# Mixing by pairs of output channels, and every transpose copied out of PSUM by ScalarE, in the first pass of a spectral convolution kernel

## Chip, cores and metric

One core of a Trainium2 chip. The metric is the time of one execution on the device in microseconds; the median of several executions is compared.

## The reference, cut to what matters

The input x is 16 images of 64 channels of 256 x 256, float32. Two layers follow each other, each a residual. Only the first layer matters here:

```
v    = groupnorm(x)                       # 32 groups of 2 channels
f    = rfft2(v)[..., :32, :17]            # only 32 x 17 modes are used
core = einsum('bhixy,hioxy->bhoxy', f, w) # 4 heads, 16 -> 16 channels per mode, complex
x    = x + irfft2(core padded with zeros) + bias
```

The second layer (a hyperbolic batch norm over channels) is computed in two further passes over x, which the change does not touch.

## The kernel before, in words

The kernel makes three passes over x. The first (`stage_a`) reads each image once, takes the 32 x 17 modes of every channel by matrix products, mixes them by the weights, and keeps the sums that the norms need. The second and third (`stage_b`, `stage_c`) read x again. Each pass is a block of its own: the next one starts when the engines have finished the one before.

**Tiles and slots.** An image is Q = 8 tiles of 8 channels (2 from each head), 2 MB each, loaded by SyncE (SP) into four buffers `xt`. For tile q of image b TensorE (PE) works in *slots*. Slot (b, q) is: the row transform of tile q (`row_dft`, L249, two halves i = 0, 1 of 8 matmul records each, into `p_rows[i]`); the transposes of tile q-1 (`transposes`, L262, two halves into `p_tr[i]`); and the column transform of tile q-2 (`col_dft`, L274, into `p_cols`). Slot (b, 2) has two more steps: the first sums of image b-1 (L284, L285) before its column transform, and the second sums of image b-2 (L292, L293) after it.

**ScalarE (ACT)** takes each tile in the order of its program: squares of heads 0 and 1 (L330), copy of `p_rows[0]` (L337), squares of head 2, copy of `p_tr[1]` of the tile before (L345), squares of head 3, copy of `p_rows[1]`. After tile 7 `keep` copies the sums of squares (L362). All engines execute their own program in order.

**VectorE (DVE)** runs, in `entry(b)`, for each q: copy of `p_tr[0]` of a later tile (`copy_tr`, L385), copy of `p_cols` of tile q of image b (L391), and the mixing of *image b-1* for two output channels (`mix`): two products of 128 x 1088 (L397) and two sums over 32 (L402). After q = 7 come `finish(b-1)` (L410 to L416: energies, which release the second sums on PE), `copy_tr(b+1, 1)`, `first_norm(b)` (waits for the first sums), `second_norm(b-1)` (waits for the second sums), and `start(b)` (L467 to L476: the normalised modes `xh` of image b), at whose end `mean_sum(b-1)` (L445 to L448) waits for two powers that GpSimd (POOL, L533, L534) computes from `second_norm`'s result.

**Who waits for whom.** `transposes(b, q)` half i waits until the copy of the tile before out of `p_tr[i]` is done (`tr_sb[i]`) and for `rows_sb`; `row_dft` half i waits for the copy of that half of the tile before; `col_dft` waits for both copies of its tile, and for the copy of `p_cols` two tiles back. `store_modes` stands in SP's queue between the loads of tiles 3 and 4 and waits for `finish`. The last image's mixing (8 times `mix`, `finish`, `second_norm`, `mean_sum`) runs on DVE alone when all else in the pass is done.

Of the kernel before, what the change touches and what calls it, by code (L numbers as in the profile page):

```python
# [20 lines left out]
ALU = mybir.AluOpType  # L21
ACT = mybir.ActivationFunctionType
AX_X = mybir.AxisListType.X
# [4 lines left out]
HEADS, CI = 4, 16  # L28
KX, KY = 32, 17
M2 = 2 * KY  # L30
# [64 lines left out]
def is_at(b, n):  # L95

    return isinstance(b, int) and b == n
# [47 lines left out]
def stage_a(nc, ctx, io, B):  # L145
# [3 lines left out]
    Q = C // 8  # L149
# [5 lines left out]
    tr_mm, tr_sb = sem("tr_mm"), [sem(f"tr_sb{i}") for i in range(2)]  # L155
    cols_mm, cols_sb = sem("cols_mm"), sem("cols_sb")
    sq_done, sq_kept = sem("sq_done"), sem("sq_kept")
    sums_mm, energy, stat_mm = sem("sums_mm"), sem("energy"), sem("stat_mm")
    y_ready, y_out, st_ready, st_out, chain = sem("y_ready"), sem("y_out"), sem("st_ready"), sem("st_out"), sem("chain")
# [4 lines left out]
    with ExitStack() as mem:  # L164
        sb = lambda n, s, d=FP32: mem.enter_context(nc.sbuf_tensor("a_" + n, s, d))
# [9 lines left out]
        wm = sb("wm", [128, CI, 2, CI * M2])  # L175
# [5 lines left out]
        xm = sb("xm", [128, CI, M2])  # L181
        xk = sb("xk", [128, CI, M2])
        xh = sb("xh", [128, KY, 2 * CI])
        prod = [sb(f"prod{k}", [128, 2, CI * M2]) for k in range(2)]
        y = sb("y", [128, CI, YS])
        yrot = sb("yrot", [128, CI, YS])
        t1, t2 = sb("t1", [128, CI, M2]), sb("t2", [128, CI, M2])
# [137 lines left out]
        @block.scalar  # L325
        def _(act):
            def squares(b, q, h):
                if not (is_at(b, 0) and q == 0 and h < 2):
                    act.wait_ge(sq_done, b * 32 + 4 * q + h - 1)
                nc.scalar.activation(junk[h % 2][:].rearrange("p (i w) -> p i w", i=2), xt[q % NX][:, h], ACT.Square,  # L330
                                     accum_out=sq[:, q, h:h + 1]).then_inc(sq_done, 1)

            def copy_rows(b, q, i):
                act.wait_ge(rows_mm, b * 16 + 2 * q + i + 1)
                if not (is_at(b, 0) and q < 2):
                    act.wait_ge(tr_mm, b * 16 + 2 * q + i - 3)
                nc.scalar.activation(rows[q % 2][i][:], p_rows[i][:], ACT.Copy).then_inc(rows_sb, 1)  # L337

            def copy_tr(b, q):
                if q < 0:  # L340
                    b, q = b - 1, q + Q
                act.wait_ge(tr_mm, b * 16 + 2 * q + 2)
                if not (is_at(b, 0) and q < 2):
                    act.wait_ge(cols_mm, b * 8 + q - 1)
                nc.scalar.activation(cols[q % 2][1][:], p_tr[1][:], ACT.Copy).then_inc(tr_sb[1], 1)  # L345

            def tile(b, q):
                act.wait_ge(x_in[q % NX], b * 64 + (q // NX) * 32 + 32)
                squares(b, q, 0)
                squares(b, q, 1)  # L350
                copy_rows(b, q, 0)
                squares(b, q, 2)
                if not (is_at(b, 0) and q == 0):
                    copy_tr(b, q - 1)
                squares(b, q, 3)
                copy_rows(b, q, 1)

            def keep(b):
                act.wait_ge(sq_done, b * 32 + 32)
                if not is_at(b, 0):  # L360
                    act.wait_ge(sums_mm, b)
                nc.scalar.activation(sqk[:], sq[:], ACT.Copy).then_inc(sq_kept, 1)  # L362
                act.wait_ge(sq_kept, b + 1)

            for q in range(Q):
                tile(0, q)
            keep(0)
            with act.Fori(1, B) as b:
                for q in range(Q):
                    tile(b, q)  # L370
                keep(b)
            copy_tr(B - 1, Q - 1)

        @block.vector
        def _(dve):
# [1 line left out]
            row = lambda k, n=16: sm[:, k, 0:n]  # L377
            pair = lambda a: a.rearrange("p (g i) -> p g i", i=2)
            V = nc.vector

            def copy_tr(b, q):
                dve.wait_ge(tr_mm, b * 16 + 2 * q + 1)
                if not (is_at(b, 0) and q < 2):
                    dve.wait_ge(cols_mm, b * 8 + q - 1)
                V.tensor_copy(cols[q % 2][0][:], p_tr[0][:]).then_inc(tr_sb[0], 1)  # L385

            def copy_cols(b, q):
                dve.wait_ge(cols_mm, b * 8 + q + 1)
# [4 lines left out]
            def mix(q, waited=None):  # L393


                for o in (2 * q, 2 * q + 1):
                    ch.inc(V.tensor_tensor(prod[o % 2][:], wm[:, o], xh[:].rearrange("p k n -> p (k n)").unsqueeze(1).to_broadcast((128, 2, CI * M2)), ALU.mult))  # L397
                ch.wait()
                for o in (2 * q, 2 * q + 1):
                    if waited is not None and o == 0:  # L400
                        dve.wait_ge(y_out, waited)
                    ch.inc(V.tensor_reduce(y[:, o, 0:M2].rearrange("p (a k) -> p a k", a=2), prod[o % 2][:].rearrange("p a (k n) -> p a k n", k=KY), AX_X, ALU.add))  # L402
                ch.wait()

            def finish(b):

                bc = lambda k: mode_w[:, k].unsqueeze(1).to_broadcast((128, CI, M2))
                if not is_at(b, 0):
                    dve.wait_ge(yrot_out, b * 16)
                V.tensor_scalar(yrot[:, :, 0:KY], y[:, :, KY:M2], misc[:, 5:6], None, ALU.mult).then_inc(y_ready, 1)  # L410
                V.tensor_scalar(yrot[:, :, KY:M2], y[:, :, 0:KY], misc[:, 6:7], None, ALU.mult).then_inc(y_ready, 1)
                ch.inc(V.tensor_tensor(t1[:], y[:, :, 0:M2], bc(0), ALU.mult))
                ch.step(V.tensor_tensor(t2[:], xk[:], bc(1), ALU.mult))
                ch.step(V.tensor_tensor(t1[:], t1[:], t2[:], ALU.add))
                ch.step(V.tensor_tensor(t1[:], t1[:], y[:, :, 0:M2], ALU.mult))
                V.tensor_reduce(row(8), t1[:], AX_X, ALU.add).then_inc(energy, 1)  # L416
# [25 lines left out]
            def mean_sum(b):  # L442
                dve.wait_ge(st_ready, b * 2 + 2)

                ch.step(V.scalar_tensor_tensor(out=row(17, 8), in0=row(13, 8), scalar=0.5, in1=pair(st[:, 0])[:, :, 0], op0=ALU.mult, op1=ALU.mult))  # L445
                a = pair(row(20))
                ch.inc(V.tensor_tensor(a[:, :, 0], a[:, :, 0], row(17, 8), ALU.add))
                ch.step(V.tensor_tensor(a[:, :, 1], a[:, :, 1], row(17, 8), ALU.subtract))  # L448
# [16 lines left out]
            def start(b):  # L465

                ch.inc(V.tensor_copy(row(2, 8), row(26, 8)))  # L467
                ch.inc(V.tensor_copy(row(3), row(27)))
                ch.step(V.tensor_copy(xk[:], xm[:]))
                dve.wait_ge(rstd1_ready, b + 1)  # L470
                ch.inc(V.tensor_tensor(xh[:].rearrange("p k (g j) -> p g j k", j=4), xk[:].rearrange("p i m -> p (i m)").rearrange("p (g j k) -> p g j k", j=4, k=KY),
                                       row(22, 8).unsqueeze(2).unsqueeze(3).to_broadcast((128, 8, 4, KY)), ALU.mult))
                ch.step(V.tensor_tensor(row(7, 8), row(4, 8), row(22, 8), ALU.mult))
                ch.step(V.tensor_scalar(row(7, 8), row(7, 8), misc[:, 4:5], None, ALU.mult))
                dcs = pair(xh[:, 0, 0::2])
                ch.step(V.tensor_tensor(dcs, dcs, row(7, 8).unsqueeze(2).to_broadcast((128, 8, 2)), ALU.add))  # L476
                if not is_at(b, 0):
                    mean_sum(b - 1)

            ch.inc(V.memset(row(20), 0.0))  # L480
            ch.inc(V.memset(y[:, :, M2:YS], 0.0))
            ch.inc(V.memset(yrot[:, :, M2:YS], 0.0))
            dve.wait_ge(const_in, 32 + 16 * 8)
            copy_tr(0, 0)
            for q in range(Q):
                copy_tr(*((0, q + 1) if q + 1 < Q else (1, 0)))
                copy_cols(0, q)
                if q == 5:
                    dve.wait_ge(w_in, 16)
                    neg = wm[:, :, 0].rearrange("p o (n r) -> p o n r", r=2)[:, :, :, 1]  # L490
                    ch.inc(V.tensor_scalar(neg, neg, -1.0, None, ALU.mult))
# [2 lines left out]

            def entry(b, last=False):
                for q in range(Q):
                    if q and not (last and q + 1 == Q):
                        copy_tr(*((b, q + 1) if q + 1 < Q else (b + 1, 0)))
                    copy_cols(b, q)
                    mix(q, None if is_at(b, 1) or q else (b - 1) * 16)  # L500
                finish(b - 1)
                if not last:
                    copy_tr(b + 1, 1)
                first_norm(b)
                second_norm(b - 1)
                start(b)

            copy_tr(1, 1)
            entry(1)
            with dve.Fori(2, B - 1) as b:  # L510
                ch.loop(b, 2, PER_A)
# [2 lines left out]
            entry(B - 1, last=True)  # L514
            for q in range(Q):
                mix(q, None if q else (B - 1) * 16)
            finish(B - 1)
            second_norm(B - 1)
            mean_sum(B - 1)
# [33 lines left out]
            pool.wait_ge(macc_out, 16)  # L553


PER_A = 63

TB = 4096
TC = 2048
# [823 lines left out]
```

## Time and profile before

| what | value |
|---|---|
| median of 3 runs | 3675.0 us (3665.37 to 3679.16) |
| profiled execution, its own time | 3669.49 us |
| its span (first to last instruction) | 3667.9 us |
| PE / DVE / ACT busy over the span | 2923.4 (80%) / 2747.2 (75%) / 2096.8 us (57%) |
| first pass ends, second begins | 1131.7 us |
| products of the mixing, L397 | 256 of 1283 ns |
| sums of the mixing, L402 | 256 of 1281 ns |

The span is 1.6 us shorter than the execution's own time. Busy shares are averages over three passes with different limits; only the first pass is touched. In the rows below the start of an instruction (or of a merged run of alike ones, "xN") comes first, then its length, both in microseconds; what stands in brackets is the idle time of the engine before it and what ended it. PE's L249, L262 and L274 are each one run per slot, so that a slot can be read off as the distance between two L249 rows.

### The profile page before, as it was taken

How to read it: one execution, taken by the hardware profiler on the slowest of the kernel's cores; microseconds unless marked ns; L12 is line 12 of the kernel's file. 1: busy time of each engine (PE TensorE's matmuls, PEld its weight loads, DVE VectorE, ACT ScalarE, POOL GpSimd, SP SyncE). 2: the span in 40 equal slices, each digit the busy share in tenths (PEclk: the TensorE clock that was granted, in tenths of full speed). 3: DMA queues.
4: the chain of work that ended last, by engine and by line, in shares of the span. 5: the costliest groups of instructions: out<-in, count | busy, mean ns of one | idle time of the engine just before them, and what ended most of it. 6: DMA issues, size and time to landing. Idle time of an engine off the chain costs nothing. (4 is left out here: it accounts for less than half of the span.)

```text
span 3667.9 us, 70122 instructions
## 1 busy us (share of the span) xinstructions
PE 2923.4 (80%) x26018; PEld 1461.4 (40%) x26018; DVE 2747.2 (75%) x2984; ACT 2096.8 (57%) x2866; POOL 1512.5 (41%) x862
## 2 busy tenths in 40 slices
PE   6998888989843766776775498898888899888887
PEld 3555555555521221222221344444444444444443
DVE  1888888888886546544564398888888888888888
ACT  5776676767720011101111388787777787777787
POOL 0101011010111111111111287787777777777778
PEclk9998888988866888887787699999999999999999
DMA  9877767777716989999996599999999999999998
GB/s 379 298 265 258 277 244 290 258 277 274 248 64 224 400 326 391 400 397 387 403 399 221 177 391 382 380 376 374 371 368 368 368 378 376 370 381 373 370 386 341
DMA packets 293210, 1211.32 MB, mean 330 GB/s; under 512 B 35266, under 2 KB 49799, under 8 KB 210695
## 3 DMA queue, kind: packets, MB, share of 16 engines
q1 hardware_dynamic: 263526, 1152.42, 82.5%
q0 software_dynamic: 14112, 43.37, 3.6%
q10 hardware_dynamic: 15360, 12.60, 1.2%
q8 instruction: 148, 2.42, 0.3%
q14 instruction: 64, 0.52, 0.0%
HBM read 883.89 MB, written 324.31 MB: 329 GB/s over the span
## 5 line engine op out<-in xcount | busy, mean ns | idle before, releaser
L1309 POOL TENSOR_TENSOR c_ot<-c_ot,c_pp 128x1024 f32<-128x1024 f32 x512 | 1213.6, 2372 | 411.2 <-DVE c_ot L1262 410.0
L1252 DVE SCALAR_TENSOR_TENSOR c_xt<-c_xt,keep_k,c_p_u 128x1024 f32<-128x1024 f32 x512 | 653.7, 1277 | 135.8 <-PE c_p_u L1132 109.5
L1262 DVE SCALAR_TENSOR_TENSOR c_ot<-c_p_f,keep_k,c_xt 128x1024 f32<-128x1024 f32 x512 | 657.3, 1284 | 108.3 <-DMA out<-c_ot 59.8
L1206 ACT ACTIVATE c_pp<-c_p_p,keep_cols 128x1024 f32<-128x1024 f32 x512 | 570.7, 1115 | 259.8 <-PE c_p_p L1144 258.7
L1132 PE MATMUL c_p_u<-c_mv,c_zc 64*128 64x256 f32 x4096 | 595.6, 410 | 78.9 <-DVE c_xt L1252 76.9
L1213 ACT ACTIVATE c_sq<-c_xt,keep_cols 128x1024 f32<-128x1024 f32 x512 | 583.1, 1139 | 63.9 <-DVE c_xt L1252 63.6
L330 ACT ACTIVATE a_junk<-a_xt 128x1024 bf16<-128x1024 f32 x512 | 537.1, 1053 | 29.1 <-DMA a_xt<-in_x 21.8
L249 PE MATMUL a_p_rows<-a_xt,a_dft_h 128*64 128x512 f32 x2048 | 516.3, 650 | 32.8 <-DMA a_bias_t<-in_bias 18.1
L1132 PEld LDWEIGHTS c_p_u<-c_mv,c_zc 64*128 64x128 f32 x4096 | 361.1, 190 | 362.7 <-issue 219.5
L528 POOL TENSOR_TENSOR a_sm<-a_sm 128x8 f32<-128x8 f32 x16 | 26.7, 1670 | 929.4 <-DVE a_sm L463 929.4
L1144 PE MATMUL c_p_f<-c_rt,keep_lw 64*128 64x512 bf16 x1024 | 315.3, 388 | 104.6 <-DVE c_ot L1262 95.8
L667 PE MATMUL b_p_al<-b_xt,b_awc 128*32 128x512 f32 x2048 | 290.0, 642 | 95.7 <-DMA b_xt<-in_x 95.7
L402 DVE TENSOR_REDUCE a_y<-a_prod 128x34 f32<-128x1088 f32 x256 | 317.5, 1281 | 5.7
L1144 PE MATMUL c_p_p<-c_rt,keep_lw 64*128 64x512 bf16 x1024 | 318.5, 392 | 0.0
L397 DVE TENSOR_TENSOR a_prod<-a_wm,a_xh 128x1088 f32<-128x1088 f32 x256 | 317.9, 1283 | 0.3
L1155 PE MATMUL c_p_t<-c_sq,c_hw 128*32 128x512 f32 x2048 | 289.3, 638 | 1.3 <-ACT c_sq L1213 1.3
L828 DVE TENSOR_TENSOR b_prod<-b_spt,b_arow 64x2176 f32<-64x2176 f32 x16 | 38.7, 2418 | 330.1 <-DMA b_spt<-spec 330.0
L725 ACT ACTIVATE b_dn<-b_dn,b_minus 128x512 f32<-128x512 f32 x16 | 11.6, 722 | 478.3 <-DVE b_dn L853 478.3
L667 PE MATMUL b_p_ls<-b_xt,b_awc 128*32 128x512 f32 x2048 | 279.5, 621 | 0.0
L1118 PEld LDWEIGHTS c_p_z<-c_idft,c_ys 128*37 128x37 f32 x7936 | 232.2, 114 | 106.0 <-issue 106.0
L1118 PE MATMUL c_p_z<-c_idft,c_ys 128*37 128x64 f32 x7936 | 271.2, 221 | 0.0
L274 PE MATMUL a_p_cols<-a_dft_w,a_cols 128*128 128x34 f32 x2048 | 264.4, 288 | 3.1 <-DVE a_xm L391 3.1
(206 smaller groups left out, 2964.1 us busy)
## 6 DMA issues: line engine op xcount, KB each, us to landing
a_xt<-in_x SPq DMA_DIRECT2D x256, 1024.0 KB, 8.1
b_xt<-in_x SPq DMA_DIRECT2D x128, 2048.0 KB, 16.8
c_xt<-in_x SPq DMA_DIRECT2D x256, 1024.0 KB, 15.9
out<-c_ot SPq DMA_DIRECT2D x256, 1024.0 KB, 16.3
c_rt<-maps SPq DMA_DIRECT2D x256, 96.0 KB
maps<-b_maps ACTq DMA_DIRECT2D x192, 64.0 KB, 13.7
maps<-b_maps POOLq DMA_DIRECT2D x64, 192.0 KB, 10.0
dmap<-b_dmap POOLq DMA_DIRECT2D x16, 768.0 KB, 13.2
```

The source lines that it names most:

```text
L249: last = nc.tensor.matmul(p_rows[i][64 * t:64 * t + 64, :], dft_h[:, j], xt[q % NX][:, t::2, i, j * W:(j + 1) * W], start=(j == 0), stop=( ...
L330: nc.scalar.activation(junk[h % 2][:].rearrange("p (i w) -> p i w", i=2), xt[q % NX][:, h], ACT.Square, accum_out=sq[:, q, h:h + 1]).then_ ...
L397: ch.inc(V.tensor_tensor(prod[o % 2][:], wm[:, o], xh[:].rearrange("p k n -> p (k n)").unsqueeze(1).to_broadcast((128, 2, CI * M2)), ALU.m ...
L667: last = nc.tensor.matmul(out[32 * j:32 * j + 32, :], awc[:, par, kind, 15 - k:47 - k], xt[t % NX][:, at:at + 512], start=(k == 0), stop=F ...
L1118: last = nc.tensor.matmul(p_z[64 * at:64 * at + YS, 64 * c:64 * c + 64], ys[:, 8 * part + c], idft[:, chunk, at], start=True, stop=True)
L1132: last = nc.tensor.matmul(p_u[:, 512 * at + W * r:512 * at + W * r + W], zc[t // CH][64 * at:64 * at + 64, i], mv[t % NB][64 * at:64 * at ...
L1144: last = nc.tensor.matmul(p[:, 512 * k:512 * k + 512], keep["lw"][at:at + 64, b].rearrange("p c s -> p (c s)"), rt[t % NB][at:at + 64, c:c ...
L1206: S.activation(pp[n][:], p_p[:], ACT.Identity, bias=keep["cols"][:, b, 1:2]).then_inc(pp_done, 1)
L1213: S.activation(sq[t % 2][:, 1024 * n:1024 * n + 1024], xt[t % NB][:, 1024 * n:1024 * n + 1024], ACT.Square, scale=keep["cols"][:, b, 0:1]) ...
L1252: V.scalar_tensor_tensor(out=u, in0=u, scalar=kc, in1=p_u[:], op0=ALU.mult, op1=ALU.add).then_inc(u_done, 1)
L1262: V.scalar_tensor_tensor(out=ot[t % NB][:, at], in0=p_f[:], scalar=kinv, in1=xt[t % NB][:, at], op0=ALU.add, op1=ALU.mult).then_inc(f_done, 1)
L1309: P.tensor_tensor(o, o, pp[n][:], ALU.add).then_inc(o_done, 1)
```

## The change

Three edits in `stage_a`. (1) `mix` handles two output channels with one product of 128 x 2176 and one sum, in place of two and two; `prod` becomes one buffer of the same total size. (2) DVE's `copy_tr` is gone; ACT's takes the half i as an argument, and a tile on ACT is now: squares 0, squares 1, rows 0, **tr 0**, squares 2, **tr 1**, squares 3, rows 1. (3) `mean_sum` leaves the end of `start`; `mean_sum(b-2)` now follows the first `mix` of `entry(b)`.

```diff
-        prod = [sb(f"prod{k}", [128, 2, CI * M2]) for k in range(2)]
+        prod = sb("prod", [128, 2, 2, CI * M2])
 ...
-            def copy_tr(b, q):
+            def copy_tr(b, q, i):
                 if q < 0:
                     b, q = b - 1, q + Q
-                act.wait_ge(tr_mm, b * 16 + 2 * q + 2)
+                act.wait_ge(tr_mm, b * 16 + 2 * q + i + 1)
                 if not (is_at(b, 0) and q < 2):
                     act.wait_ge(cols_mm, b * 8 + q - 1)
-                nc.scalar.activation(cols[q % 2][1][:], p_tr[1][:], ACT.Copy).then_inc(tr_sb[1], 1)
+                nc.scalar.activation(cols[q % 2][i][:], p_tr[i][:], ACT.Copy).then_inc(tr_sb[i], 1)
             def tile(b, q):
                 squares(b, q, 0)
                 squares(b, q, 1)
                 copy_rows(b, q, 0)
+                if not (is_at(b, 0) and q == 0):
+                    copy_tr(b, q - 1, 0)
                 squares(b, q, 2)
                 if not (is_at(b, 0) and q == 0):
-                    copy_tr(b, q - 1)
+                    copy_tr(b, q - 1, 1)
                 squares(b, q, 3)
                 copy_rows(b, q, 1)
 ...
             def mix(q, waited=None):
-                for o in (2 * q, 2 * q + 1):
-                    ch.inc(V.tensor_tensor(prod[o % 2][:], wm[:, o], xh[:].rearrange("p k n -> p (k n)").unsqueeze(1).to_broadcast((128, 2, CI * M2)), ALU.mult))
-                ch.wait()
-                for o in (2 * q, 2 * q + 1):
-                    if waited is not None and o == 0:
-                        dve.wait_ge(y_out, waited)
-                    ch.inc(V.tensor_reduce(y[:, o, 0:M2].rearrange("p (a k) -> p a k", a=2), prod[o % 2][:].rearrange("p a (k n) -> p a k n", k=KY), AX_X, ALU.add))
-                ch.wait()
+                over = xh[:].rearrange("p k n -> p (k n)").unsqueeze(1).to_broadcast((128, 4, CI * M2))
+                ch.step(V.tensor_tensor(prod[:].rearrange("p o a n -> p (o a) n"), wm[:, 2 * q:2 * q + 2].rearrange("p o a n -> p (o a) n"), over, ALU.mult))
+                if waited is not None and q == 0:
+                    dve.wait_ge(y_out, waited)
+                ch.step(V.tensor_reduce(y[:, 2 * q:2 * q + 2, 0:M2].rearrange("p o (a k) -> p o a k", a=2), prod[:].rearrange("p o a (k n) -> p o a k n", k=KY), AX_X, ALU.add))
 ...
             def start(b):
 ...
-                if not is_at(b, 0):
-                    mean_sum(b - 1)
 ...
             def entry(b, last=False):
                 for q in range(Q):
-                    if q and not (last and q + 1 == Q):
-                        copy_tr(*((b, q + 1) if q + 1 < Q else (b + 1, 0)))
                     copy_cols(b, q)
                     mix(q, None if is_at(b, 1) or q else (b - 1) * 16)
+                    if q == 0 and not is_at(b, 1):
+                        mean_sum(b - 2)
                 finish(b - 1)
-                if not last:
-                    copy_tr(b + 1, 1)
                 first_norm(b)
                 second_norm(b - 1)
                 start(b)
```

The DVE `copy_tr` before the loop goes too, and the last image's eight `mix` calls get the same `mean_sum` after the first.

## Rows read from the trace of the kernel before

**Rows 1.** Granted clock, DMA share and GB/s in the first pass: the last three columns of a window.

```profile
0.00:1131.70 1131.70, 918.02 (x5248) 548.78 (x5248) 892.48 (x1397) 738.10 (x1425) 134.46 (x72) 0.85 0.71 254
```

**Rows 2.** Who waited for whom between 150 and 900 us: total, times, longest.

```profile
PE a_p_tr L262 <- DVE a_cols L385: 53.5, 12, 4.5
DVE a_sm L445 <- POOL a_st L534: 48.2, 12, 4.1
```

**Rows 3.** Timeline of PE, the second sums (L292): first, fourteenth, fifteenth and last.

```profile
156.81 0.60 PE L292 MATMUL a_p_stat<-a_sm,a_sel 128*128 128x16 f32 x2 [2.76 <-DVE a_sm L416]
...
1000.58 0.60 PE L292 MATMUL a_p_stat<-a_sm,a_sel 128*128 128x16 f32 x2 [2.76 <-DVE a_sm L416]
...
1063.38 0.61 PE L292 MATMUL a_p_stat<-a_sm,a_sel 128*128 128x16 f32 x2 [8.07 <-DVE a_sm L416]
...
1117.99 0.61 PE L292 MATMUL a_p_stat<-a_sm,a_sel 128*128 128x16 f32 x2 [53.57 <-DVE a_sm L416]
```

**Rows 4.** Timeline of PE through the turn of one image; start, length, idle before.

```profile
352.91 5.47 PE L249 MATMUL a_p_rows<-a_xt,a_dft_h 128*64 128x512 f32 x16
...
361.04 3.65 PE L249 MATMUL a_p_rows<-a_xt,a_dft_h 128*64 128x512 f32 x16
369.17 1.97 PE L262 MATMUL a_p_tr<-a_ident,a_rows 128*128 128x128 f32 x8 [4.48 <-DVE a_cols L385]
...
374.33 5.00 PE L249 MATMUL a_p_rows<-a_xt,a_dft_h 128*64 128x512 f32 x16
...
381.99 3.65 PE L249 MATMUL a_p_rows<-a_xt,a_dft_h 128*64 128x512 f32 x16
385.57 1.09 PE L262 MATMUL a_p_tr<-a_ident,a_rows 128*128 128x128 f32 x8
...
388.31 3.65 PE L249 MATMUL a_p_rows<-a_xt,a_dft_h 128*64 128x512 f32 x16
```

**Rows 5.** Timeline of DVE in the same period.

```profile
347.64 0.36 DVE L410 TENSOR_SCALAR a_yrot<-a_y,a_misc 128x272 f32<-128x272 f32 x1
...
361.96 0.17 DVE L445 SCALAR_TENSOR_TENSOR a_sm<-a_sm,a_st 128x8 f32<-128x8 f32 x1 [4.01 <-POOL a_st L534]
...
368.42 0.69 DVE L385 COPY a_cols<-a_p_tr 128x512 f32<-128x512 f32 x1 [0.20 <-DVE a_y L402]
369.03 0.22 DVE L391 COPY a_xm<-a_p_cols 128x68 f32<-128x68 f32 x1
...
407.36 0.23 DVE L391 COPY a_xm<-a_p_cols 128x68 f32<-128x68 f32 x1 [0.24 <-PE a_p_cols L274]
...
412.54 0.36 DVE L410 TENSOR_SCALAR a_yrot<-a_y,a_misc 128x272 f32<-128x272 f32 x1
```

**Rows 6.** Timeline of ACT, one tile and the turn of the image.

```profile
386.78 0.60 ACT L345 ACTIVATE a_cols<-a_p_tr 128x512 f32<-128x512 f32 x1 [0.60 <-PE a_p_tr L262]
387.27 1.05 ACT L330 ACTIVATE a_junk<-a_xt 128x1024 bf16<-128x1024 f32 x1
...
388.31 0.59 ACT L337 ACTIVATE a_rows<-a_p_rows 128x512 f32<-128x512 f32 x1
388.79 1.06 ACT L330 ACTIVATE a_junk<-a_xt 128x1024 bf16<-128x1024 f32 x1
...
395.11 0.23 ACT L362 ACTIVATE a_sqk<-a_sq 128x32 f32<-128x32 f32 x1
395.84 1.06 ACT L330 ACTIVATE a_junk<-a_xt 128x1024 bf16<-128x1024 f32 x1 [0.50 <-ACT a_sqk L362]
```

**Rows 7.** Groups of instructions of the second pass, DVE: count, busy us, mean ns.

```profile
L831 DVE TENSOR_REDUCE b_vm<-b_prod 64x34 f32<-64x2176 f32 x16 | 67.7, 4233 | 0.5
...
L828 DVE TENSOR_TENSOR b_prod<-b_spt,b_arow 64x2176 f32<-64x2176 f32 x16 | 38.7, 2418 | 330.1 <-DMA b_spt<-spec 330.0
```

**Rows 8.** Busy time, clock, DMA share and GB/s of two stretches of the period.

```profile
355.50:361.20 5.70, 5.70 (x38) 3.61 (x36) 2.29 (x10) 3.32 (x7) 5.31 (x2) 0.90 1.05 396
402.00:408.00 6.00, 6.00 (x42) 3.61 (x38) 5.48 (x7) 5.41 (x12) 0.00 (x0) 1.00 0.05 19
```

More of the change, by code:

```diff
@@ L371, in _ @@
                 keep(b)
-            copy_tr(B - 1, Q - 1)
+            for i in range(2):
+                copy_tr(B - 1, Q - 1, i)
         @block.vector
@@ L379, in _ @@
             V = nc.vector
[L381 to L385, printed above, removed]
             def copy_cols(b, q):
@@ L483, in _ @@
             dve.wait_ge(const_in, 32 + 16 * 8)
-            copy_tr(0, 0)
             for q in range(Q):
-                copy_tr(*((0, q + 1) if q + 1 < Q else (1, 0)))
                 copy_cols(0, q)
@@ L506, in entry @@
                 start(b)
-            copy_tr(1, 1)
             entry(1)
@@ L516, in _ @@
                 mix(q, None if q else (B - 1) * 16)
+                if q == 0:
+                    mean_sum(B - 2)
             finish(B - 1)
@@ L553, in _ @@
             pool.wait_ge(macc_out, 16)
-PER_A = 63
+PER_A = 47
 TB = 4096
```

## Prediction

> **What bounds the kernel now.** I read the page first for the passes: nothing of the change lies behind 1131.7 us, so all is decided in the first pass. There PE, DVE and ACT are busy 918, 892 and 738 of 1131.7 us, at DMA share 0.71 and granted clock 0.85 [rows 1]: no engine is full and the clock has dips. So some order of work, and not one engine, sets the pace. The waits name two points: PE waits at a transpose for DVE's copy, 12 times for up to 4.5 us, and DVE waits at `mean_sum` for POOL, 12 times for up to 4.1 us [rows 2]. The second sums on PE give the rhythm: the reader is to see that they start at 156.81 and at 1000.58 us, thirteen images later, each time after 2.76 us of idleness: 64.9 us an image [rows 3].
>
> Then I followed one image (5, between two second sums) on PE [rows 4]. From the second sums at 351.95 (352.91 less the 0.96 us of the sums) PE runs slot (5,3), whose row transform takes 5.40 us to its transposes instead of 3.58, because the engine is at the 1.2 GHz level for part of it. Slot (5,4) begins at 361.04; after its row transform PE stands for 4.48 us, until DVE's copy that starts at 368.42 [rows 5] frees `p_tr[0]`. After this stall transposes and columns take 5.16 us (369.17 to 374.33) instead of 2.74, and the next row transform about 4.93 instead of 3.58. The last full slots are 6.32 us apart (381.99 to 388.31) with no gap: there PE is the bound. The reason for the stall is in DVE's order: the modes `xh` are ready at 357.95, `mean_sum` waits 4.01 us until 361.96, then copy, products and sums of the first `mix`, and only then the copy that PE needs [rows 5].
>
> **A check of this reading.** Take the period without the stall. From one second sums to the start of slot 4: 361.04 - 351.95 = 9.09. Six slots, (b,4) to (b+1,1), of 6.32: 37.92. After the last, DVE copies (0.11 later) and mixes: 407.36 to 412.54 is 5.18. `finish` up to the next second sums: 351.95 - 347.64 = 4.31 [rows 4, 5]. Sum 56.6. The stall and its slow clock: 4.48 + (5.16 - 2.74) + (4.93 - 3.58) = 8.25. Together 64.9, as measured [rows 3].
>
> **The change part by part.**
>
> *Copies to ACT.* The stall with its 8.25 us goes: `p_tr[0]` is now freed by ACT, which is not held by `mean_sum` or `mix`. What is late next is the same loop without the stall, and PE's wait of 2.76 us for `finish` stays, since both its sides start from the same column transform: DVE needs 5.1 + 4.3, PE 6.7 for slot (b,2). So the low clock behind it stays too.
>
> Price on ACT: one copy more per tile, 0.49 us from its start to the next (386.78 to 387.27); squares take 1.04, rows copies 0.48 [rows 6]. A tile is 4 x 1.04 + 2 x 0.48 + 2 x 0.49 = 6.10 us, under 6.32. But the new copy waits for the transposes with squares 2, tr 1, squares 3 and rows 1 queued behind it, and rows 1 is what half 1 of PE's next row transform waits for. That ring: from the transposes' start to the first copy about 0.80 (the copy of the second half starts 1.21 after them, 385.57 to 386.78, and a half of them is 0.41), 0.49, 1.04, 0.49, 1.04, the rows copy 0.59 in full, about 0.05 to PE, and half a row transform, 1.79: 6.3 us. It is level with the slot; I take 0 for it, and up to 0.15 a slot for the range. `keep` takes 0.73 us once an image (395.11 to 395.84) [rows 6]; ACT's slack in a tile is 0.22, so 0.5 us of it reaches PE, inside the six slots. I take 0.5.
>
> *Products and sums by pairs.* Copy, two products and two sums take 5.18 us (407.36 to 412.54) [rows 5]; less about 0.14 for the copy a pair is 2.52, handover included. The second pass has one product of 2176 elements per partition at 2418 ns [rows 7], 2.46 with the same handover. So 0.06 us each for products and sums, 0.13 per `mix`, 1.0 us an image. For the sums no row has this form with contiguous reads; the nearest by size takes 4233 ns [rows 7], but reads its input across rows, whereas here 32 neighbours are summed as in the present 1281 ns. Bounds 2.42 and 4.23, and I take 2.42. DVE then needs per image: from the second sums to `xh` 5.4 (357.95 - 351.95, less 0.6 for the copy that goes), eight times 5.1 for copy and mixing, `finish` 4.3, `mean_sum` 0.5: 51.0 of the new period. The saving is hidden under PE except in the one `mix` after the last slot, 0.13.
>
> The Trainium skill, page "VectorE: DVE Perf Modes", section "The DRAIN you can't avoid", says that an instruction on VectorE starts only when the one before has emptied the pipe. By that a merged pair saves a whole start, two times 1283 less 2418 or 0.15 us, in place of the 0.06 above, and the time would come out 1 to 2 us lower, in the last image's mixing alone.
>
> *`mean_sum`.* Its 4.0 us wait is taken off DVE. At its new place it comes 5.4 + 5.1 = 10.5 us behind the second sums, and POOL's result is there at 361.96 - 351.95 = 10.0: no wait, with half a microsecond to spare. If POOL were 1 us later under the mixing, DVE's 6 us of slack take it. In the steady images this edit brings nothing beyond the copies, since both remove the same stall.
>
> **The sum.** Period: 56.6 - 0.13 + 0.5 = 57.0, against 64.9: 7.9 x 13 = 102.7.
> The period from 1000.58 to 1063.38 (62.8) has the same stall, and no further image: 9.1 + 4 slots (25.3) to the columns of tile 5, from there DVE alone: three times 5.05, `finish` 4.3: 53.9. Saves 8.9.
> From there to 1117.99 (54.6) DVE works alone [rows 3]: the wait of 4.1 and 8 x 0.13 go: 5.1.
> Before 156.81 no such stall stands: 0.
> In all 116.7. Span 3667.9 - 116.7 = 3551.2, own time 3552.8. The median of the runs before lies 5.5 above the profiled one and the lowest 4 below; I add some 2 us: 3555.
>
> **The rivals.**
>
> *ACT's ring is longer than a slot.* For it: it is level within what I can read. Against: the wait from transposes to copy is measured. At 0.4 us a slot: 13 x 6 x 0.4 = 31 us back, 3586.
>
> *The clock.* The first row transform after the second sums runs low for about half its length in this trace. Had it run at full clock, 1.8 us an image less: 3531; all of it low, 1.8 more: 3578 [rows 4]. The Trainium skill, page "TensorE: Matmul & The Clock Gate", section "Part 1: The HAM clock gate", says that the point at which the clock rises depends on where in the monitor's own window the work begins, and varies from run to run. By it the dip's length is open, though the old trace repeats it at every image.
>
> *DMA becomes the bound.* Tiles 4 to 6 queue behind `store_modes` and come in a burst, at 396 GB/s, and the queue then runs dry, 19 GB/s [rows 8]. An image is 17.4 MB with its stores: 44 us at 396 GB/s, of 57. Against: there is a rest in every period. If the loads ran at 330 the image took 53 us plus the blocked queue, 6 us by that row and some more: about 61, 4 x 14 = 56 us back, 3611.
>
> *The sums run slowly: slower than before.* In place DVE's sum over 128 x 2176. At 4.23 us a `mix` with its copy is 6.9, an image 8 x 6.9 + 10.4 = 65.6 on DVE alone, +0.7 x 13; the next two periods +2.8 and +10.9: 3669.5 + 23 = 3692. It decides from 4.04 us on; below that the kernel is faster. Against: 32 contiguous floats, as now.
>
> *The change doesn't do what it says:* another wait keeps PE at slot 4 (the copy of `p_cols`, say). DVE reaches that copy 5.4 us behind the second sums and PE needs it 14 behind. Little speaks for it: 3665.
>
> **How the numbers follow.** Forecast 0.64 (its own range 3540 to 3570), ACT's ring 0.13, clock 0.12, DMA 0.04, no effect 0.03, slow sums 0.04. The range runs from the clock's lower end to the ring's upper one: 3533 to 3590. A measurement of this kernel tells some 0.5% (18 us) from no change. Faster by more than that: the first four, 0.93; same 0.03; slower 0.04.
>
> **What would show it.** Second sums 57 us apart, still with a 2.8 us wait; no wait at a transpose longer than 0.6 us; slots of 6.3 us; one sum at 2.42 us; `mean_sum` without a wait; ACT waiting at the first transpose copy for 0.2 us in a steady tile; the second pass beginning near 1015 us. I am wrong if slots are 6.6 or more (ring), if the row transforms wait for x (DMA), or if the sum takes over 3 us.

## The result, and the profile after

The changed kernel takes 3572.3 us (median, 3570.42 to 3573.87), the one before 3670.55 (four executions: the three of the table above and one more): ratio 0.973, 95% interval 0.9707 to 0.9753. The forecast was 3555 with 3533 to 3590: the mechanism as told, the time 17 us above it. The profiled span is 3572.3 us, 95.6 less than before; the second pass begins at 1030.4 us, 101 earlier than before, where the forecast had it near 1015.

The second sums on PE, first, fourteenth, fifteenth and last (against [rows 3]):

```profile
157.47 0.60 PE L292 MATMUL a_p_stat<-a_sm,a_sel 128*128 128x16 f32 x2 [2.67 <-DVE a_sm L410]
...
910.89 0.60 PE L292 MATMUL a_p_stat<-a_sm,a_sel 128*128 128x16 f32 x2 [2.61 <-DVE a_sm L410]
...
966.71 0.61 PE L292 MATMUL a_p_stat<-a_sm,a_sel 128*128 128x16 f32 x2 [7.95 <-DVE a_sm L410]
...
1016.60 0.61 PE L292 MATMUL a_p_stat<-a_sm,a_sel 128*128 128x16 f32 x2 [48.85 <-DVE a_sm L410]
```

Thirteen periods from 157.47 to 910.89 are 753.4 us, 57.96 each, against 64.9 before. The wait ahead of each is still there, 2.61 us. The last two stretches are 55.8 and 49.9, against 62.8 and 54.6.

PE, the row transforms behind the first two second sums, then the turn of a later image (against [rows 4]):

```profile
158.43 5.98 PE L249 MATMUL a_p_rows<-a_xt,a_dft_h 128*64 128x512 f32 x16
...
216.01 6.20 PE L249 MATMUL a_p_rows<-a_xt,a_dft_h 128*64 128x512 f32 x16
...
366.09 3.68 PE L249 MATMUL a_p_rows<-a_xt,a_dft_h 128*64 128x512 f32 x16
...
372.43 1.94 PE L249 MATMUL a_p_rows<-a_xt,a_dft_h 128*64 128x512 f32 x8
...
374.65 1.94 PE L249 MATMUL a_p_rows<-a_xt,a_dft_h 128*64 128x512 f32 x8 [0.28 <-ACT a_rows L337]
...
379.25 3.68 PE L249 MATMUL a_p_rows<-a_xt,a_dft_h 128*64 128x512 f32 x16
...
389.68 6.41 PE L249 MATMUL a_p_rows<-a_xt,a_dft_h 128*64 128x512 f32 x16
...
396.02 1.09 PE L262 MATMUL a_p_tr<-a_ident,a_rows 128*128 128x128 f32 x8
```

In the images between 150 and 900 us no transpose waits for a copy any more; slot 4 starts 10.0 us after the second sums and the slots follow without a gap. A plain slot is 6.34 us (366.09 to 372.43). The one with `keep` in it is cut in two by a wait of 0.28 for ACT and lasts 6.82 (372.43 to 379.25). But the row transform behind the second sums, at 389.68, needs 6.34 us to its transposes, where [rows 4] had 5.40: it is slow almost throughout. The two windows show the clock that was granted to it and to the slot after:

```profile
389.70:394.50 4.80, 4.80 (x13) 1.46 (x14) 4.01 (x22) 0.60 (x1) 4.09 (x2) 0.50 1.04 398
398.70:405.00 6.30, 6.30 (x42) 3.62 (x41) 5.87 (x7) 6.17 (x13) 1.96 (x2) 1.00 1.05 386
```

0.50, then 1.00: the 1.2 and the 2.4 GHz level. Compare the three long rows: 5.98, 6.20 and 6.41 us. The periods begin with 57.58 and 57.79 and rise to 58.02, where they stay.

The groups of the mixing on DVE, and who waits for whom between 150 and 900 us (against [rows 2]):

```profile
L397 DVE TENSOR_REDUCE a_y<-a_prod 128x68 f32<-128x2176 f32 x128 | 309.9, 2421 | 5.6
L394 DVE TENSOR_TENSOR a_prod<-a_wm,a_xh 128x2176 f32<-128x2176 f32 x128 | 309.3, 2416 | 0.3
```

```profile
DVE a_xm L388 <- PE a_p_cols L274: 82.7, 64, 1.8
...
PE a_p_stat L292 <- DVE a_sm L410: 34.0, 13, 2.7
...
PE a_p_rows L249 <- ACT a_rows L337: 3.7, 13, 0.3
DVE a_sm L439 <- POOL a_st L522: 3.1, 13, 0.2
```

One product and one sum of 2176 elements take 2416 and 2421 ns. DVE now waits for PE's columns, and at `mean_sum` for POOL only 0.2 us.

### The profile page after: what moved, and what is told of

Read it like the earlier page. It is cut to its first block and busy times, and to the rows that moved or that the text cites. A ratio compares the mean times of both kernels' runs of the same rounds, so it can differ in the third digit from the quotient of the medians.

```text
span 3572.3 us, 69803 instructions
## 1 busy us (share of the span) xinstructions
PE 2887.4 (81%) x26018; PEld 1418.3 (40%) x26018; DVE 2648.6 (74%) x2600; ACT 2158.7 (60%) x2994; POOL 1541.4 (43%) x862
## 3 DMA queue, kind: packets, MB, share of 16 engines
q8 instruction: 148, 2.42, 0.3%
## 5 line engine op out<-in xcount | busy, mean ns | idle before, releaser
L397 DVE TENSOR_REDUCE a_y<-a_prod 128x68 f32<-128x2176 f32 x128 | 309.9, 2421 | 5.6
L394 DVE TENSOR_TENSOR a_prod<-a_wm,a_xh 128x2176 f32<-128x2176 f32 x128 | 309.3, 2416 | 0.3
L249 PEld LDWEIGHTS a_p_rows<-a_xt,a_dft_h 128*64 128x64 f32 x2048 | 136.4, 147 | 307.9 <-issue 187.9
```

What stands on the lines that cost most here:

```text
L249: last = nc.tensor.matmul(p_rows[i][64 * t:64 * t + 64, :], dft_h[:, j], xt[q % NX][:, t::2, i, j * W:(j + 1) * W], start=(j == 0), stop=( ...
```

## Experiments

The first three do one edit each on the kernel before; the others start from the changed kernel. Times are medians; the kernel before was run beside them on the same chip and is given with each group.

**Edit 1 alone, pairs.** The diff is the `mix` and `prod` part of the change.

> The kernel before with edit 1 alone (products and sums by pairs); copies and mean_sum as before. Forecast: DVE saves 0.13 us per mix, but only two mixes of an image lie on the path (the last one before finish and the first one before the copy that PE waits for): 2 x 0.13 x 14 + 1.0 for the last image, some 5 us less than before, second sums 64.6 us apart. Rival: all 128 mixes count, 16 us less.

Measured: 3684.2 us (before: 3675.6), ratio 1.004 with 1.000 to 1.008. No gain: the forecast of 64.6 us a period and some 5 us less missed, and so did its rival. PE at the second sums and behind them:

```profile
353.45 0.60 PE L292 MATMUL a_p_stat<-a_sm,a_sel 128*128 128x16 f32 x2 [2.63 <-DVE a_sm L413]
...
354.41 5.71 PE L249 MATMUL a_p_rows<-a_xt,a_dft_h 128*64 128x512 f32 x16
```

The wait is 2.63 us, 0.13 less than in [rows 3], as one `mix` is 0.13 shorter. But the row transform after it is 5.71 long against 5.47 in [rows 4], and the period settles at 64.85, as before. The same happens at the stall of slot 4: it is 4.13 us (4.48 before), and the row transform behind it takes 5.23 us to its transposes (4.93 before). Only in the last image, where DVE works alone, does the edit show: 53.6 us against 54.6. The last second sums come at 1118.3 us, before at 1118.0, so the time above is that of the later passes, which this edit doesn't touch and whose length in this run I can't explain.

**Edit 3 alone, `mean_sum`.**

> The kernel before with edit 3 alone (mean_sum after the first mix); DVE keeps its copies. Forecast: the 4.0 us wait of DVE goes, so the copy that PE waits 4.5 us for comes 4.5 us earlier and the stall at slot 4 with its low clock goes as well: period 57 to 58.5 us (DVE alone needs 6.0 + 8 x 5.8 + 0.5 + 4.3 = 57.2), time 3570 to 3585, nearly the whole gain of the change. Rival: the edits add up and this one brings only the wait itself, 4.1 us x 15: 3610.

Measured: 3580.0 us (before: 3675.6), ratio 0.975 (0.9735 to 0.9774); the period is 58.37. The stall at slot 4 is down to half a microsecond (1.2 at most):

```profile
331.87 0.60 PE L292 MATMUL a_p_stat<-a_sm,a_sel 128*128 128x16 f32 x2 [3.83 <-DVE a_sm L416]
...
332.83 5.62 PE L249 MATMUL a_p_rows<-a_xt,a_dft_h 128*64 128x512 f32 x16
...
345.25 1.09 PE L262 MATMUL a_p_tr<-a_ident,a_rows 128*128 128x128 f32 x8 [0.49 <-DVE a_cols L385]
...
566.31 4.93 PE L249 MATMUL a_p_rows<-a_xt,a_dft_h 128*64 128x512 f32 x16
...
578.74 1.09 PE L262 MATMUL a_p_tr<-a_ident,a_rows 128*128 128x128 f32 x8 [1.18 <-DVE a_cols L385]
```

DVE is now the bound (its copies are still on it): between 150 and 900 us it waits for PE once, for 0.2 us. The last two lines, four images on, show it from PE's side: the row transform behind the second sums is 0.69 us shorter, PE waits 0.69 us longer for DVE's copy, and the period is the same. So here the length of the slow stretch costs nothing. This edit alone gives 95.6 us, the next one alone 94.1, and the whole change 98.3 (95.2 where it was run again). That the edits don't add up is settled.

**Edit 2 alone, copies.**

> The changed kernel with mean_sum put back to the end of start and the mixing by single channels again (edit 2 alone). Forecast: DVE needs 5.4 + 4.5 + 8 x 5.2 + 4.3 = 55.8 us an image, under the 57.9 of the changed kernel, so the period stays at 57.9 and only the last two images, where DVE works alone, pay 4 + 5 us: 3580 to 3585. Rival: the wait at mean_sum counts in every image, 4 us x 14 back: 3628.

Measured: 3581.4 us (before: 3675.6), ratio 0.978 (0.971 to 0.984), as forecast; the period is 58.02, the last stretch 54.6. One of the four runs took 3618 us, hence the wide interval; the argument rests on the trace.

```profile
DVE a_sm L442 <- POOL a_st L524: 52.4, 13, 4.1
...
PE a_p_stat L292 <- DVE a_sm L413: 35.7, 13, 2.8
```

DVE waits 4 us at `mean_sum` in each image (52.4 us in 13), and it costs nothing until the last image: each of the two edits removes the stall by itself, and whichever comes second brings almost nothing.

**The second sums later on PE.**

```diff
 def slot(b, q):
     row_dft(b, q)
+    if q == 3 and not (is_at(b, 0) or is_at(b, 1)):
+        second_sums(b - 2)
     transposes(*before(b, q, 1))
...
-    if q == 2 and not (is_at(b, 0) or is_at(b, 1)):
-        second_sums(b - 2)
```

> The changed kernel with the second sums on PE moved from the end of slot 2 to behind the row transform of slot 3. Forecast: PE has 3.6 us of work while DVE finishes, so its 2.6 us wait and the low clock behind it (the row transform of 6.3 us for 3.6) both go; period 52 to 53 us (PE 8 x 6.34 + 0.8 + 0.5, DVE about 52), 14 x 5.3 = 74 us less than the changed kernel: 3498. Rival: another limit sits right under (ACT's ring with keep, or the loads): period 55 or more, 3530 or more.

Measured: 3564.6 us (before: 3675.6), ratio 0.970 (0.967 to 0.974). My forecast of 3498 missed by 67 us, and the rival was right (another limit, here the loads; the periods are 56.0 to 57.95):

```profile
211.90 3.65 PE L249 MATMUL a_p_rows<-a_xt,a_dft_h 128*64 128x512 f32 x16
...
215.48 0.40 PE L292 MATMUL a_p_stat<-a_sm,a_sel 128*128 128x16 f32 x2
...
216.86 1.87 PE L274 MATMUL a_p_cols<-a_dft_w,a_cols 128*128 128x34 f32 x16
...
221.79 6.23 PE L249 MATMUL a_p_rows<-a_xt,a_dft_h 128*64 128x512 f32 x16 [3.05 <-DMA a_xt<-in_x]
```

The second sums no longer wait (215.48 follows 211.90 at once), and slot 3 runs at full clock. But slot 4 then waits 3.05 us for the load of x, and its row transform takes 6.15 us, as slowly as before. The wait and its slow clock have moved one slot on; the wait is there in every image, 2.4 to 3.1 us. In the changed kernel the same load was hidden behind them.

**The same, and the stores later.**

```diff
-    if q == 4:
+    if q == 6:
         store_modes(b - 2)
     load(b, q)
```

> As sums_later, and store_modes in SP's queue moved from behind the load of tile 3 to behind the load of tile 5. Theory: sums_later kept a period of 57 us because store_modes held the load of tile 4 until DVE's finish, so PE waited 3.1 us for x and its clock fell there in place of at the second sums. With the loads released: period 52 to 53 us, 3495 to 3505. Rival: the loads are short of bandwidth (17.4 MB in 52 us are 335 GB/s): waits for x remain, 3530 or more.

Measured: 3497.6 us (before: 3673.7), ratio 0.952 (0.950 to 0.954). The forecast held. The period is 52.03 to 52.09:

```profile
362.57 3.65 PE L249 MATMUL a_p_rows<-a_xt,a_dft_h 128*64 128x512 f32 x16
...
366.15 0.40 PE L292 MATMUL a_p_stat<-a_sm,a_sel 128*128 128x16 f32 x2
...
369.33 3.67 PE L249 MATMUL a_p_rows<-a_xt,a_dft_h 128*64 128x512 f32 x16
```

Row transform, second sums, the rest of the slot and the next one follow without a gap, 362.57 to 369.33 in 6.76. So it was the order in SP's queue, `store_modes` ahead of the load of tile 4, that made x late. This version beats both kernels, the changed one by 75 us.

**The second rows copy ahead of the transposes on ACT**, on top of that.

```diff
     copy_rows(b, q, 0)
-    if not (is_at(b, 0) and q == 0):
-        copy_tr(b, q - 1, 0)
     squares(b, q, 2)
+    copy_rows(b, q, 1)
     if not (is_at(b, 0) and q == 0):
+        copy_tr(b, q - 1, 0)
         copy_tr(b, q - 1, 1)
     squares(b, q, 3)
-    copy_rows(b, q, 1)
```

> As sums_and_stores_later, and ACT's order in a tile is squares 0, squares 1, rows 0, squares 2, rows 1, tr 0, tr 1, squares 3, so that the second rows copy no longer stands behind the transposes. If ACT's ring is what makes a slot 6.34 and lets keep through with 0.5 us, slots are 6.32 and keep costs nothing: 0.5 to 0.7 us an image less than sums_and_stores_later, 8 to 11 us. Rival: DVE (51 us an image and its wait at the second sums) is then the bound: under 4 us.

Measured: 3500.7 us (before: 3673.7), ratio 0.9545 (0.9505 to 0.9585); the period is 52.1 (one of 53.1). Nothing was gained where the forecast had 8 to 11 us; the rival is right. Slots are 6.32 us and no wait for rows copies is left, so ACT's ring (the copies of the transposes, with the second rows copy behind them, for which PE's next slot waits) was what gave 6.34 and let `keep` through; but PE now waits for DVE at the second sums, and DVE for PE's columns no more:

```profile
PE a_p_stat L292 <- DVE a_sm L409: 5.7, 10, 0.6
...
DVE a_xm L387 <- PE a_p_cols L274: 0.2, 1, 0.2
```

DVE is the bound there.

**The same with single channels.** The `mix` of the kernel before in the last one.

> rows_first with edit 1 undone (two products and two sums per mix). In rows_first DVE waits for nobody in an image and is the bound at 52.1 us. Theory: the 0.13 us per mix now counts in full: period 53.1, and 1.0 in the last image: 14 x 1.0 + 1 = 15 us more than rows_first, 3515. Rival: pairs bring nothing on DVE (starts are hidden by overlap): 3500.

Measured: 3514.0 us (before: 3676.0), ratio 0.959 (0.954 to 0.9635). Beside the run before (3500.7) that is 13 us, near the forecast, but not quite by its sum: the periods are not 53.1 throughout, they go 53.07, 54.70, 52.66 in turn, 53.5 in the mean. In the long ones the low clock is back (granted clock 0.52 between 424 and 430 us), behind a shorter wait than that of the changed kernel:

```profile
422.79 0.39 PE L292 MATMUL a_p_stat<-a_sm,a_sel 128*128 128x16 f32 x2 [1.58 <-DVE a_sm L412]
...
427.43 5.47 PE L249 MATMUL a_p_rows<-a_xt,a_dft_h 128*64 128x512 f32 x16
```

So of 1.37 us an image some 1.03 are the products and sums themselves (8 x 0.13), and the rest comes with the low clock. In the traces the first pass is 17.5 us longer; the medians, from two chips, are 13 apart. In the kernel before, pairs were worth nothing that shows.

**The wait filled with work.**

```diff
+    for n in range(3):
+        nc.tensor.matmul(p_stat[0:64, 128:512], dft_h[:, 0],
+            sel[:].rearrange("p a n -> p (a n)")[:, 0:384], start=True, stop=True)
     second_sums(b - 2)
```

> The changed kernel with three matmuls of 384 columns (float32, into unused columns of the second sums' bank, result not used) on PE between the column transform of slot 2 and the wait for the second sums. They take about 1.9 us and lie in the wait of 2.6 us. Theory (the low clock comes from PE's having nothing to do there): the row transform behind it falls from 6.3 towards 3.6 us, period about 55.5, 3540. Rival (the low clock has another reason): nothing changes, 3572; if the added work delays the second sums, slower.

Measured: 3534.8 us (before: 3673.7), ratio 0.963 (0.9595 to 0.9666), as the theory had it. More work on PE, 37 us less than the changed kernel:

```profile
375.22 2.15 PE L306 MATMUL a_p_stat<-a_sel,a_dft_h 128*64 128x384 f32 x6
...
377.90 0.39 PE L292 MATMUL a_p_stat<-a_sm,a_sel 128*128 128x16 f32 x2 [0.53 <-DVE a_sm L412]
...
378.44 3.65 PE L249 MATMUL a_p_rows<-a_xt,a_dft_h 128*64 128x512 f32 x16
```

The row transform behind is 3.65 us, the full clock, and the period 54.8 to 55.2. The extra matmuls lie in the wait for DVE, so they take nothing; what they give back is the slow stretch, 2.8 us in the row transform and 0.4 in the second sums themselves (0.54 us for 0.96). So the low clock comes from PE's having too little to do ahead of it.

**`finish` longer.**

```diff
 ch.step(V.tensor_tensor(t2[:], xk[:], bc(1), ALU.mult))
+ch.step(V.tensor_tensor(t2[:], xk[:], bc(1), ALU.mult))
```

> The changed kernel with one product of finish made twice (0.76 us more on DVE between the last mix and the second sums, which PE waits for). Plain chain: every period is 0.76 us longer, in all 3572 + 15 x 0.76 = 3583. Rival, from the period of 57.97 us that image after image keeps in the changed kernel although its first row transforms differ: the stretch at the low clock gets shorter by as much as the wait gets longer, the period stays within 0.2 us: 3573 to 3576.

Measured: 3574.8 us (before: 3673.7), ratio 0.973 (0.971 to 0.9755). The second sums of one image:

```profile
388.16 0.60 PE L292 MATMUL a_p_stat<-a_sm,a_sel 128*128 128x16 f32 x2 [3.36 <-DVE a_sm L411]
...
389.12 5.64 PE L249 MATMUL a_p_rows<-a_xt,a_dft_h 128*64 128x512 f32 x16
```

The plain chain had 3583, its rival 3573 to 3576: the rival is right. The wait is 3.36 us, 0.75 longer; the row transform behind it 5.64, 0.77 shorter than the 6.41 of the changed kernel; and the period 58.02, the same to 0.01 us. The shorter stretch at the low clock makes up for what is put on the chain ahead of it.

**The stores later alone**, the `q == 6` edit on the changed kernel.

> The changed kernel with only store_modes moved behind the load of tile 5. Theory: in the changed kernel PE reaches tile 4 later than its load lands, so the store costs nothing there and its move brings nothing: period 58.0, 3570 to 3575. Rival: the queue held by store_modes already costs the changed kernel time: up to 3 us an image less, 3530.

Measured: 3578.2 us (before: 3676.0), beside 3580.8 for the changed kernel on that chip; period 58.02. In the changed kernel the load is hidden, so the move brings nothing: it pays only once the second sums have moved.

**The changed kernel again.**

> The changed kernel unaltered, as a base for the others on the same chip. Period 57.6 to 58.03 us as in its first trace if the stretch at low clock evens it out; 57.0 to 58.5 and uneven if not. 3572.

Measured: 3580.8 us (before: 3676.0), ratio 0.976 (0.972 to 0.979). The periods are 57.54, 57.76, 57.90, 57.96, 57.99 and then 58.01 to 58.03: the sequence of the first trace within 0.05 us. The profiled executions of the two are 4 us apart, and those lie behind the first pass.

## Why the prediction was right, and where its 17 us are

**What bounded it: right.** Either cure of the stall at slot 4 brings the period to 58, as `mean_sum` alone and the copies alone show. Its size holds too: 8.25 us for stall and slow clock and 0.13 for the `mix` go; 0.48 for `keep`, 0.12 for six slots of 6.34 instead of 6.32, and 0.94 of slow clock (below) come back. That leaves 6.84; the period fell by 64.9 - 57.96 = 6.94.

**The terms of the period.** The wait ahead of the second sums stays: forecast 2.76, measured 2.61. ACT's ring: forecast level with the slot, measured 6.34 for 6.32, and the experiment with the rows copy first names it as the cause. `keep`: forecast 0.5, measured 6.82 - 6.34 = 0.48. Pairs: 2416 and 2421 ns, forecast 2.42. `mean_sum` at its new place: forecast no wait, measured 0.2. Loads: not the bound, as forecast.

**The term that was mis-sized** is the slow clock behind the second sums. I took its length from [rows 4], 5.40 us for the row transform, and had its longer form as a rival. Measured: 6.34, so 0.94 an image, half of what that rival had. It is nearly all of the 0.96 between the 57.0 of the forecast and the 57.96 measured. The main forecast's own range, 3540 to 3570, was missed by 2 us; only the wider one, which has the rivals in it, holds 3572. The account of the difference, from the span:

| term | forecast | measured | difference, us |
|---|---|---|---|
| 13 periods | 57.0 | 57.96 | 12.4 |
| next stretch | 53.9 | 55.8 | 1.9 |
| last stretch | 49.5 | 49.9 | 0.4 |
| up to the first second sums | 156.8 | 157.5 | 0.7 |
| from the last ones to the end | 2549.9 | 2555.7 | 5.8 |

Together 21.2, on 3551.2: 3572.4, against a span of 3572.3. The medians are only 17 apart because I had added 2 us to the forecast, and because the median lies 1.6 below the profiled execution. In the fourteenth stretch half is the slow clock; most of the rest is a wait that the forecast left out. ACT's second rows copy is late, PE waits for it, and DVE for PE's columns:

```profile
948.03 0.98 PE L262 MATMUL a_p_tr<-a_ident,a_rows 128*128 128x128 f32 x4 [1.20 <-ACT a_rows L337]
...
952.38 0.23 DVE L388 COPY a_xm<-a_p_cols 128x68 f32<-128x68 f32 x1 [0.89 <-PE a_p_cols L274]
```

The last line of the table lies in passes that the change doesn't touch; what made them longer is open.

**Why the low stretch grew.** The experiments show that its length is no constant of the kernel: a longer `finish` shortened it by as much (0.77 for 0.75), a shorter `mix` lengthened it (5.71 from 5.47), and the period stayed where it was, 58.02 in four kernels (the changed one, the stores later, the copies alone and the longer `finish`, the last two with other work on DVE) and 64.85 in two. So I should have read the 64.9 of [rows 3] not as a sum of terms alone, but as a value at which sum and clock settle. The trace of before shows this settling: its first periods are 65.1 us, and they shrink to 64.85 while the row transform behind the second sums shrinks from 5.57 to 5.35. What value another chain settles at, no row of before could tell. It holds only where the slow stretch lies on the path: with `mean_sum` alone DVE is the bound, and the stretch goes from 5.91 down to 4.87 and back up to 6.39 at a period of 58.37. That the period settles is shown; the mechanism in the chip behind it is not.

The Trainium skill's page "TensorE: Matmul & The Clock Gate", section "Part 1: The HAM clock gate", has the rise depend on where in the monitor's own window the work begins. The trace is in line with it: the same work takes 5.98, 6.20 and 6.41 us at different starts. But the section also calls the ramp "run-variable", and in this kernel one further run repeats the sequence of the periods to 0.05 us.

By the Trainium skill's page "VectorE: DVE Perf Modes", section "The DRAIN you can't avoid", as the prediction read it, each pair merged would save 0.15 us. The same section adds that a next instruction that is not held starts earlier, and the trace agrees with that: two products of 1283 ns take 2.48 us together. The last image, with DVE alone, gives 54.6 - 53.6 = 1.0 us for 16 pairs, 0.064 each: the forecast's 0.06 holds.

## What to carry to other kernels

When one wait can be removed in two ways, they don't add up: price the loop that is left and ask which of the edits still lies on it. A short wait on TensorE costs twice if the clock has fallen behind it; here 2.6 us of idleness and the slow row transform behind it were worth 75 us, once the work was put in an order in which no queue (PE's own, then SP's) held something that wasn't ready. And when a step is taken off a loop, look at what was hidden behind it: the late load of tile 4 cost nothing until the second sums stopped waiting.

## What the runs showed that I hadn't expected

The period of a loop with such a wait is not the sum of its parts: adding 0.75 us to DVE left it at 58.02 us, taking 0.13 us off left it at 64.85. A change to such a loop can measure as nothing though each instruction does what it should. Pairs showed their worth only where DVE is the bound (52.1 us an image against 53.5), and even there a part of the difference is the low clock, back in every third image. And idle time filled with useless matmuls made the kernel 37 us faster.
